# Query and key projection of the next tile as three rounded products, with the tile split by ScalarE and VectorE

## What is computed

```python
# layer 0: attention over the 1024 columns of a tile; init is the context
q = einsum('dc,bct->btd', Wq, init) + bq        # 64 features
k = einsum('dc,bct->bdt', Wk, init) + bk
attention = softmax(einsum('btd,bds->bts', q, k))
v = einsum('oc,bct->bto', Wv, layernorm(x)) + bv
x = x + einsum('bts,bsc->bct', attention, v)
# layer 0: feed-forward with signs for weights, input and output scaled by a softmax of 8 experts
x = x + ((xf * in_scale) @ sign(weight).T) * out_scale + bias
# layer 1: attention of the 128 rows of x over the 128 rows of the context
Q = layernorm(x) @ Wq.T + bq;  K = ctx @ Wk.T + bk
x = x + softmax(Q @ K.T / 32) @ ctx
# layer 1: low-rank mixture of 8 experts of rank 16
x = x + 2 * (low * 8 * softmax(router)) @ B
```

## Time and profile before

| | us |
|---|---|
| median of 3 runs | 2157.5 (2156.91 to 2157.81) |
| the profiled execution | 2157.1 |
| its span in the trace | 2154.9 |
| TensorE busy | 2125.2 |
| VectorE busy | 1855.1 |
| ScalarE busy | 1159.6 |
| GpSimd busy | 260.2 |

### The profile page before, as it was taken

One profiled execution on the slowest core, in us unless ns is written; L12 is line 12 of the kernel. 1 busy time (PEld: TensorE's weight loads), 2 busy tenths in 40 slices (PEclk: granted clock), 3 DMA queues, 4 the chain that ended last, 5 costly groups with the idle time before them and its releaser, 6 DMA issues.

```text
span 2154.9 us, 35721 instructions
## 1 busy us (share of the span) xinstructions
PE 2125.2 (99%) x11503; PEld 1668.6 (77%) x11503; DVE 1855.1 (86%) x3102; ACT 1159.6 (54%) x1721; POOL 260.2 (12%) x302
## 2 busy tenths in 40 slices
PE   9979999999999999999999999999999999999998
PEld 7857777778777777787777778777777787777777
DVE  9268899888889998888898988888998888898984
ACT  4145555655555565555555655555566555555651
POOL 0001111111111111111111111101110111111100
PEclk9999999999999999999999999999999999999999
DMA  6344333333433323334343333443323334343310
GB/s 220 139 156 127 118 124 98 96 129 119 136 123 130 110 89 112 127 127 136 117 127 102 97 122 124 129 135 118 112 94 105 127 127 136 117 134 101 96 50 30
DMA packets 110874, 254.03 MB, mean 118 GB/s; under 512 B 12976, under 2 KB 14272, under 8 KB 110848
## 3 DMA queue, kind: packets, MB, share of 16 engines
q1 hardware_dynamic: 110848, 253.69, 36.5%
HBM read 215.89 MB, written 20.97 MB: 110 GB/s over the span
## 4 chain that ended last, share of the span: by engine, by line
PE 91%; DVE 1%; ACT 1%; issue 0%; POOL 0%; DVEq 0%; POOLq 0%; ACTq 0%
PE acc L1213 17%; PE shared L1142 7%; PE scores L1162 6%; PE acc L1173 6%; PE shared L1187 6%; PE acc L1176 6%; PE acc L1174 6%; PE shared L1188 5%; PE scores L1202 5%; PE scores L1201 5%; PE shared L1394 3%; PE shared L1320 3%; PE scores L1148 2%; PE scores L1343 2%; PE scores L1350 1%; PE shared L1263 1%
## 5 line engine op out<-in xcount | busy, mean ns | idle before, releaser
L1005 DVE TENSOR_TENSOR p_lo<-prob,p_hi 128x1024 fp32r<-128x1024 f32 x256 | 312.1, 1219 | 103.7 <-ACT p_hi L791 85.9
L784 ACT ACTIVATE prob<-scores 128x1024 f32<-128x1024 f32 x256 | 260.7, 1018 | 236.6 <-PE scores L1202 185.3
L882 DVE TENSOR_REDUCE neg_max<-scores 128x1 f32<-128x1024 f32 x256 | 306.7, 1218 | 42.2 <-PE scores L1162 40.8
L697 POOL TENSOR_TENSOR rstd<-var_eps,minus_half 128x1 f32<-128x1 f32 x128 | 126.0, 984 | 1747.7 <-DVE var_eps L872 1747.7
L791 ACT ACTIVATE p_hi<-prob 128x1024 fp32r<-128x1024 f32 x256 | 271.4, 1060 | 42.7 <-PE acc L1213 38.5
L1173 PE MATMUL acc<-m_hi,cT_hi 128*128 128x512 f32 x512 | 217.3, 424 | 3.6 <-DVE cT_lo L1071 2.7
L1187 PE MATMUL shared<-signT,y_hi 128*128 128x512 f32 x512 | 205.5, 401 | 0.0
L1176 PE MATMUL acc<-m_ring,cT_hi 128*128 128x512 f32 x512 | 202.9, 396 | 0.0
L1201 PE MATMUL scores<-q_hl,k_hh 128*128 128x512 f32 x512 | 201.1, 393 | 1.8 <-DVE q_m L987 1.4
L1174 PE MATMUL acc<-m_hi,cT_lo 128*128 128x512 f32 x512 | 202.3, 395 | 0.0
L1202 PE MATMUL scores<-q_m,k_l 128*128 128x512 f32 x512 | 202.1, 395 | 0.0
(11 more groups left out here) (222 smaller groups left out, 4214.4 us busy)
## 6 DMA issues: line engine op xcount, KB each, us to landing
m_ring<-m_low SPq DMA_DIRECT2D x512, 256.0 KB, 3.1
c_in<-in_ctx SPq DMA_DIRECT2D x32, 512.0 KB, 3.3
xn<-in_x SPq DMA_DIRECT2D x32, 512.0 KB, 4.1
x<-in_x SPq DMA_DIRECT2D x32, 512.0 KB, 3.2
c_val<-in_ctx SPq DMA_DIRECT2D x32, 512.0 KB, 3.7
out_x<-oscale SPq DMA_DIRECT2D x32, 512.0 KB, 3.0
q_m<-q_hl SPq DMA_DIRECT2D x32, 256.0 KB, 3.1
k_hh<-k_hh SPq DMA_DIRECT2D x32, 256.0 KB, 3.5
```

The lines of the kernel that those rows point to most:

```text
L882: nc.vector.tensor_reduce(neg_max[:, t:t + 1], scores[t % 2][:, :], AX_X, ALU.max, negate=True).then_inc(row_max, 1)
L1005: nc.vector.tensor_tensor(p_lo[s % 2][:, :], prob[s % 2][:, :], p_hi[s % 2][:, :].bitcast(F32), ALU.subtract).then_inc(p_lo_ready, 1)
```

## The change

The projection weight is split in the setup: wqk_hi is the rounded wqkT, wqk_lo its remainder (VectorE, group "small"). The context tile is split in each iteration: c_hi by ScalarE at s=4 behind p_hi, c_lo by VectorE at s=6 behind p_sum. The projection becomes six rounded products: for each half of the columns wqk_hi with c_hi and wqk_lo with c_hi, then, behind a wait for c_lo, wqk_hi with c_lo for both halves. c_hi lies in the place of oscale, and c_lo in that of q_hl, whose last reader is the score product of s=7; so c_hi waits for the transposes of xn_2 and c_lo for the last scores.

The half h=1 of the turned keys goes from VectorE (s=4) to ScalarE, as four activations of 128x128 with a column of the key bias each, at s=5 between exp and p_hi. attnT shares its place with lowT_lo, so ScalarE's write to it also waits for out_done of the tile before.

```diff
-        wqkT = sb("wqkT", [P, P])
+        wqk_hi = sb("wqk_hi", [P, P], F32R)
+        wqk_lo = sb("wqk_lo", [P, P], F32R)
@@ VectorE, setup
-                            nc.vector.tensor_copy(wqkT[:, :], s[:, 0:P])
-                            last = nc.vector.tensor_copy(wvT[:, :], s[:, P:2 * P])
+                            nc.vector.tensor_copy(wqk_hi[:, :], s[:, 0:P]).then_inc(b_hi_made, 1)
+                            nc.vector.tensor_copy(wvT[:, :], s[:, P:2 * P])
+                            dve.wait_ge(b_hi_made, 1)
+                            last = nc.vector.tensor_tensor(wqk_lo[:, :], s[:, 0:P], wqk_hi[:, :].bitcast(F32), ALU.subtract)
@@ buffers
-        oscale = sb("oscale", [P, D])
+        with ExitStack() as before:
+            oscale = sb("oscale", [P, D], F32, before)
+        c_hi = sb("c_hi", [P, D], F32R)
+        c_lo = q_hl
@@ ScalarE, loop over s
                         if chain and s == 4:
                             act.wait_ge(y_lo_ready, nth(2, c, 2))
                             transposed_half(2, c)
+                        if attend and s == 5:
+                            act.wait_ge(sc1_done, nth(1, a - 1, 1))
+                            act.wait_ge(kwT_done, nth(2, a, 1))
+                            for j in range(4):
+                                last = nc.scalar.activation(kwT[:, 4 + j, :], shared[1][:, j * P:(j + 1) * P], ACT.Identity,
+                                                            bias=key_bias[:, 4 + j:5 + j])
+                            last.then_inc(kwT_ready, 1)
                         if attend:
                             act.wait_ge(exp_ready, nth(8, a, s + 1))
                             act.wait_ge(pv_done, nth(8, a, s - 1))
...
+                        if prepare and s == 4:
+                            act.wait_ge(c_loaded, nth(16, b, 16))
+                            act.wait_ge(xnT_done[2], nth(2, c, 2))
+                            nc.scalar.activation(c_hi[:, :], c_in[:, :], ACT.Identity).then_inc(c_hi_ready, 1)
...
                             act.wait_ge(att_done, nth(2, c - 1, 2))
+                            act.wait_ge(out_done, nth(2, c - 1, 2))
                             nc.scalar.activation(attnT[:, :], shared[1][:, 0:P], ACT.Identity).then_inc(attnT_ready, 1)
@@ VectorE, loop over s
-                        if attend and s in (4, 6):
-                            keys_turned(a, (6 - s) // 2)
+                        if prepare and s == 6:
+                            dve.wait_ge(c_hi_ready, nth(1, b, 1))
+                            dve.wait_ge(scores_done, nth(8, a, 8))
+                            nc.vector.tensor_tensor(c_lo[:, :], c_in[:, :], c_hi[:, :].bitcast(F32),
+                                                    ALU.subtract).then_inc(c_lo_ready, 1)
+                        if attend and s == 6:
+                            keys_turned(a, 0)
@@ TensorE, loop over s
                         if prepare and s == 7:
-                            pe.wait_ge(c_loaded, nth(16, b, 16))
+                            pe.wait_ge(c_hi_ready, nth(1, b, 1))
                             pe.wait_ge(exp_ready, nth(8, a, 7))
                             for h in range(2):
-                                mm(scores[0][:, half(h)], wqkT[:, :], c_in[:, half(h)], start=True, stop=True).then_inc(qk_done, 1)
+                                mm(scores[0][:, half(h)], wqk_hi[:, :], c_hi[:, half(h)], start=True, stop=False)
+                                mm(scores[0][:, half(h)], wqk_lo[:, :], c_hi[:, half(h)], start=False, stop=False)
+                            pe.wait_ge(c_lo_ready, nth(1, b, 1))
+                            for h in range(2):
+                                mm(scores[0][:, half(h)], wqk_hi[:, :], c_lo[:, half(h)], start=False, stop=True).then_inc(qk_done, 1)
```

More of the change, by code:

```diff
@@ L340, in _ @@
                             nc.vector.tensor_copy(hi, turned).then_inc(b_hi_made, 1)
-                            dve.wait_ge(b_hi_made, i + 1)
+                            dve.wait_ge(b_hi_made, i + 2)
                             last = nc.vector.tensor_tensor(lo, turned, hi.bitcast(F32), ALU.subtract)
@@ L510, in build @@
         gate_parts = attn
-        attnT = sb("attnT", [P, P])
+        with ExitStack() as before:
+            attnT = sb("attnT", [P, P], F32, before)
         low = attn
+        lowT_lo = sb("lowT_lo", [P, P], F32R)
         lowT_hi = sb("lowT_hi", [P, P], F32R)
-        lowT_lo = sb("lowT_lo", [P, P], F32R)
         def psum(name, shape):
@@ L535, in build @@
         qk_done = sem("qk_done")
+        c_hi_ready = sem("c_hi_ready")
+        c_lo_ready = sem("c_lo_ready")
         doubled = sem("doubled")
```

## The result

The changed kernel takes 2225.2 us (median of 4 runs, 2224.03 to 2225.73) beside 2157.2 us of the kernel before on the same chip: ratio 1.0319, 95% interval 1.0307 to 1.0331, 68 us slower. The forecast was 2224. The profiled execution took 2224.7 us, its span is 2222.9.

What follows compares the result with a forecast made beforehand. It took VectorE's nearly gapless queue and ScalarE's handovers at s=4 to s=7 to decide, not TensorE's 99%. 30 tiles at 2.2 us give 66, plus 1.4, less 0.3: 2157 + 67 = 2224 us, range 2202 to 2246.

Steps and rivals of the forecast that it cites:

- The bound: Attention steps s=4 to s=7: VectorE runs almost without a gap, TensorE is barely covered; its 99% busy share hides short stalls.
- Projection: On TensorE, six rounded products take 1.40 us against 1.72; the 0.32 us saved a tile falls into idle time.
- Keys ahead of p_hi of s=5: ScalarE's queue waits for turned kw, then four activations hold it 1.10 us; p_lo of s=5 starts 1.65 us later.
- c_hi: ScalarE's copy at s=4, 1.06 us, costs nothing because the queue's next wait covers it; 0 in k=0 too.
- c_lo: VectorE's subtraction at s=6 adds 1.13 us less 0.59 of idle; with the keys' 1.65, p_lo of s=7 comes +2.19.
- Behind the projection: Denominators' copy comes 2.19 us later, q_hl +2.25; nothing is won back before the next tile: 2.2 us a tile.
- The ends: Tiles outside k=2 to 31: k=0 costs 0, k=1 saves 0.32 us, k=32 costs +1.4 us; setup 0.
- The sum: Whole kernel: 66 + 1.4 - 0.3 = 67 us on 2157, giving 2224 us.
- A: ScalarE's 1.51 us of idle ahead of exp of s=6 takes in the keys: faster, 2147 us; chance 0.06.
- B: p_hi of s=5 comes in time, only VectorE's added work costs, 0.37 us a tile: 2168 us; chance 0.08.
- C: New stalls let TensorE's clock fall to 1.2 GHz; if in each tile, 2269 us; chance 0.04.

Runs made afterwards that it cites:

- experiment 2: The kernel before with only the half h=1 of the turned keys moved to ScalarE at s=5, fp32 projection, no c_hi or c_lo: 2205.1 us.
- experiment 7: The changed kernel with both halves of the keys on VectorE and no c_lo, the last product reading c_hi again: 2165.9 us.
- experiment 1: The changed kernel with both halves of the turned keys on VectorE again, the rest of the change kept: 2178.2 us.
- experiment 6: The changed kernel with its six rounded products made half by half, the query's first half complete behind three: 2221.7 us.
- experiment 4: The changed kernel with ScalarE's four key activations moved one place, behind p_hi of s=5 instead of ahead of it: 2186.6 us.
- experiment 8: The changed kernel with both halves of the keys on VectorE and c_lo made on GpSimd: 2244.6 us.

## Why the prediction was right

**The bound.** Right. The stretch from s=4 to the output is set by VectorE's queue and by what ScalarE hands it, though TensorE is busy 99% of the time.

**Projection.** 1.39 us instead of 1.72, as computed, and in this change worth nothing: with fp32 products the kernel is not slower (2221.6 us).

**Keys ahead of p_hi of s=5.** Right in place, order and size. The four activations held the queue 1.02 us against 1.10, between the bounds of 0.72 and 1.47. p_lo of s=5 came at 1062.19 - 30.20 = 1031.99 and not 1032.12: +1.52 against +1.65. Of the 0.13 us between them 0.08 are the activations, 0.06 a handover of 0.03 us instead of 0.09, 0.01 the kw tile, and p_hi gives 0.02 back (1.08 us instead of 1.06). The page "ScalarE: Activation LUTs" of the Trainium skill (section "What ACT_TABLE_LOAD costs") gave 1.18 us for the four as an estimate: 0.16 too much, where the row's step was 0.08 too much.

**c_hi.** Nothing in steady tiles, as said: ScalarE's idle time ahead of the keys is 1.74 us with it and 2.69 without it (experiment 2, the same wait).

**c_lo.** It advanced the queue by 1.13 us (1066.74 to 1067.87), and p_lo of s=7 lost its idle time. Forecast +2.19, measured 1068.66 - 30.20 - 1036.35 = +2.11. One thing in this step was luck of the parts: the idle time of 0.59 us that I subtracted belonged to a wait for p_hi. Without c_lo there would have been nothing to subtract (experiment 2), since ScalarE's own queue brings p_hi of s=7 1.59 us late. With c_lo VectorE is the later of the two by 0.5 us, and the subtraction holds. I had followed one queue only.

**Behind the projection.** The copy of the denominators came +2.11 (forecast 2.19), q_hl +2.37 (2.25), the first output row +2.31. The steady tile is 64.31 us, +2.24, for 2.2 of the forecast. What p_lo brought too little, the late release of the query's first half brought back: VectorE waits 0.43 us for the denominators' rows instead of 0.23. I had counted that release as later, but only on ScalarE, and not as a cost of its own; experiment 7 shows it at 0.2 to 0.3 us a tile.

**The ends.** Here single terms were wrong and their sum right by luck. k=0 and k=1 were to give 0 and -0.3 us; in the profiled execution they gave +1.0: the copy of the denominators in k=1 starts at 174.66 instead of 173.63. c_hi is on the path in k=0, where no loop over s hides it:

```profile
118.16 0.50 PE L1369 MATMUL scores<-c_hi,wqk_hi 128*128 128x512 f32 x1 [2.52 <-ACT c_hi L814]
...
120.49 1.91 PE L1168 MATMUL shared<-ident,c_in 128*128 128x128 f32 x8
```

The projection starts 1.7 us later than before (0.4 us of it because the setup's last product ends later), and the eight transposes behind it take 1.91 us where they took 1.04. I had bounded c_hi at 1.1 us and taken 0. But how much of this arrives at k=1 isn't shown: with c_hi in the same place the copy of k=1 stands at 173.53 in experiment 1, at 173.61 in experiment 6, and elsewhere between 170.7 and 177.1.

k=32 gave +1.7 us for the +1.4 of the forecast. Behind it 2.0 us came back that I had not seen. In its profiled execution the kernel before ran that stretch at a low clock, and the changed one did not (columns as the earlier trace rows, first before, then after):

```profile
2099.60:2104.60 5.00, 3.98 (x17) 3.66 (x18) 3.30 (x5) 0.13 (x1) 0.00 (x0) 0.56 0.00 0
...
2169.55:2174.55 5.00, 3.38 (x27) 3.18 (x28) 4.22 (x8) 0.53 (x3) 0.00 (x0) 1.00 0.00 0
```

**The sum.** In the profiled executions the 30 tiles k=2 to 31 added 67.3 us (forecast 66), k=0 and k=1 +1.0 (-0.3), k=32 +1.7 (+1.4), and the end -2.0 (0): 68.0 us in the spans, for a forecast of 67. The total is nearer to the forecast than its terms are: the keys too dear by 0.13 us a tile, the query's release not priced, and at the ends two misses that cancel.

**The rivals.** A fell: the idle time ahead of exp of s=6 could take in the keys only behind p_hi, and experiment 4 shows that even then they cost. B's price was wrong: c_lo alone gave 2178, not 2168. C did not occur in steady tiles (granted clock 1.00), with 1.2 us of idle for the product and 1.6 for its weight load; with 2.19 us of idle it occurs in 7 of 30 tiles (experiment 8).

Left open: whether GpSimd could make c_lo in a stretch in which VectorE reads PSUM or waits. It would need the context tile earlier, and was not tried.

## What to carry to other kernels

A busy share of 99% says what an engine does, not that cheaper work on it shortens the program; ask which queue has no gap in the stretch of the edit, and lay new work only where that queue has room. Where a wait is moved into another engine's queue, look at what stands right behind it (four activations moved by one place were worth 38.6 us). An idle time may be subtracted only after its releaser, too, has been followed through the change.

## What the runs showed of the hardware

- A subtraction with two inputs in SBUF on VectorE takes 1.22 us, and 3.40 us when it comes while GpSimd works on a subtraction of its own (2.83 us). In the kernel before GpSimd has no instruction of this size within the loop over s.
- TensorE's granted clock stayed at 1.00 in the steady tiles of the changed kernel, with 1.21 us idle in one piece and 1.86 us in all. Behind 2.19 us of idle it fell to 0.60 over 4 us in 7 of 30 tiles, and stayed at 1.00 in the other 23. In k=0 of the changed kernel, behind 2.52 us of idle and a projection of 2.3 us with a short wait in it, it fell to 0.50:

```profile
118.00:120.40 2.40, 1.86 (x6) 1.20 (x7) 1.60 (x6) 0.11 (x2) 1.65 (x2) 0.93 1.08 347
120.40:122.50 2.10, 2.10 (x11) 2.00 (x10) 0.26 (x1) 2.08 (x3) 0.00 (x0) 0.50 0.75 261
```

  That is why the transposes there took 1.91 us; the lower level is 1.2 GHz. In experiment 1, behind 2.51 us of idle and the same products, it did not fall, and they took 1.04 us:

```profile
120.20 1.04 PE L1161 MATMUL shared<-ident,c_in 128*128 128x128 f32 x8
```

  In the last iterations of the kernel before it fell to 0.56 over 5 us with no idle time above 0.83 us near it. So in these traces the length of the idle time alone does not say whether the clock falls.
- Four activations of 128x128 from PSUM with a bias column advance ScalarE's queue by 0.255 us each; one of 128x512 without a bias by 0.49 in all.
